# Interleaving the three partial products of each output tile in the Strassen-form matmuls of a LoRA + S4D kernel

## The reference, cut to what matters

```python
# layer 0: base product plus a rank-16 adapter that each of the 128 sequences picks
result = jnp.einsum('bsd,od->bso', x, base_weight) + base_bias      # 1024 x 1024 weight
h = jnp.einsum('bsd,brd->bsr', x, lora_A_w[ids]); result += jnp.einsum('bsr,bor->bso', h, lora_B_w[ids])
x = x + result
# layer 1: per head a causal convolution over the 1024 positions, plus a skip, masked by length
K = 2.0 * jnp.einsum('hn,hnl->hl', Ct, jnp.exp(P)).real
y = irfft(rfft(x, 2048) * rfft(K, 2048))[..., :1024] + x * D[:, None]
x = x + y * mask
```

## Time and profile before

| | |
|---|---|
| median of 3 runs | 1070.05 us (1069.75 to 1071.53) |
| the profiled execution's own time | 1069.73 us |
| its span, first to last instruction | 1068.0 us |
| granted clock of TensorE, mean | 1.000 |
| PE busy | 1061.2 us (99%), 8088 matmuls |
| PEld busy (overlaps PE) | 1028.8 us, 8088 loads |
| DVE busy | 848.5 us (79%) |
| ACT busy | 717.0 us (67%) |
| HBM traffic | 284.62 MB by DMA, mean 266 GB/s |

### The profile page before, as it was taken

The page is one execution under the profiler, slowest core; times in us unless marked ns, Lnnn a source line. Parts: engine busy times, 40 slices in busy tenths (PEclk is TensorE's granted clock), DMA queues, the critical chain, the costliest instruction groups (busy, mean ns, idle before and its releaser), DMA issues.

```text
span 1068.0 us, 21568 instructions
## 1 busy us (share of the span) xinstructions
PE 1061.2 (99%) x8088; PEld 1028.8 (96%) x8088; DVE 848.5 (79%) x1263; ACT 717.0 (67%) x1260; POOL 28.6 (3%) x79
## 2 busy tenths in 40 slices
PE   9999999999999999999999999999999999999998
PEld 7999999999999999999999999999989999999997
DVE  7899887878698787878778787877488888888886
ACT  5755545755747466556557467465598888888885
POOL 0000000000000000000000000000010000000000
PEclk9999999999999999999999999999999999999999
DMA  8586758688786978868785888858798978798873
GB/s 290 202 304 221 275 191 284 199 300 307 226 269 211 298 225 277 282 229 275 229 308 179 296 260 259 293 194 283 264 346 286 350 287 335 294 326 317 304 263 123
DMA packets 162586, 284.62 MB, mean 266 GB/s; under 512 B 10739, under 2 KB 125620, under 8 KB 149044
## 3 DMA queue, kind: packets, MB, share of 16 engines
q1 hardware_dynamic: 162484, 283.26, 77.1%
HBM read 193.96 MB, written 89.26 MB: 265 GB/s over the span
## 4 chain that ended last, share of the span: by engine, by line
PE 97%; DVE 1%; ACT 1%; DMA 0%; issue 0%; DVEq 0%; SPq 0%; ACTq 0%
PE acc L1810 37%; PE acc L1970 25%; PE acc L1816 18%; PE acc L1738 5%; PE acc L1782 5%; PE acc L2005 3%; PE acc L1748 2%; DMA x_raw<-x_t 0%; PE acc L1915 0%; ACT x_hi L687 0%; PE acc L1774 0%; DVE x_sb L1262 0%; ACT L845 0%; ACT L851 0%; DVE g_sb L1460 0%
## 5 line engine op out<-in xcount | busy, mean ns | idle before, releaser
L1970 PE MATMUL acc<-u_hi,f_hi 128*128 128x512 f32 (+1 forms) x320 | 128.9, 403 | 0.0
L687 ACT ACTIVATE acc<-acc 128x512 f32<-128x512 f32 x93 | 54.0, 581 | 109.4 <-PE acc L1816 109.3
L1810 PE MATMUL acc<-t_hi,v_lo 128*128 128x256 f32 x512 | 123.0, 279 | 0.0
L1810 PE MATMUL acc<-t_hi,v_hi 128*128 128x256 f32 x512 | 122.9, 279 | 0.0
L1810 PE MATMUL acc<-t_hi,w_pair 128*128 128x256 f32 x960 | 122.4, 279 | 0.0
L1970 PE MATMUL acc<-u_lo,f_hi 128*128 128x512 f32 (+1 forms) x320 | 118.4, 370 | 0.0
L1970 PE MATMUL acc<-u_hi,f_lo 128*128 128x512 f32 (+1 forms) x320 | 118.2, 369 | 0.0
L1810 PEld LDWEIGHTS acc<-t_hi,w_pair 128*128 128x128 f32 x960 | 116.9, 188 | 0.0
L687 ACT ACTIVATE t_hi<-t_raw 128x1024 fp32r<-128x1024 f32 x64 | 67.9, 1061 | 61.7 <-DVE t_raw L1220 33.0
L1105 DVE TENSOR_TENSOR t_lo<-t_raw,t_hi 128x1024 fp32r<-128x1024 f32 x64 | 78.3, 1223 | 34.3 <-ACT t_hi L687 33.9
L1810 PEld LDWEIGHTS acc<-t_hi,v_lo 128*128 128x128 f32 x512 | 96.2, 188 | 0.0
(11 more groups left out here) (205 smaller groups left out, 2673.3 us busy)
## 6 DMA issues: line engine op xcount, KB each, us to landing
w_pair<-weight_scratch SPq DMA_DIRECT2D x71, 1024.0 KB, 6.5
x_scratch<-x_sb SPq DMA_DIRECT2D x32, 1024.0 KB, 6.0
out<-out_sb SPq DMA_DIRECT2D x63, 512.0 KB, 4.8
x_raw<-x_t SPq DMA_DIRECT2D x15, 2048.0 KB, 11.1
u_raw<-x_scratch SPq DMA_DIRECT2D x14, 2048.0 KB, 11.8
wq_raw<-state_scratch SPq DMA_DIRECT2D x16, 1024.0 KB, 8.1
a_raw<-lora_a SPq DMA_DIRECT2D x128, 64.0 KB, 5.7
b_raw<-lora_b SPq DMA_DIRECT2D x128, 64.0 KB, 2.1
```

Of the source, the lines that this page charges most:

```text
L687: return act.activation(dst, src, ACT.Copy)
L1810: pe.matmul(by_row(bank_part(bank, i)), w[:, k, i, :], hi[:, k, :, :], start=opens and i == 0 and k == 0 and s == 0, stop=False, skip_grou ...
L1970: mm = pe.matmul(bank, w, m, start=first and i == 0, stop=last and i == 2, skip_group_check=onto_closed)
```

## The change

`product_hi` and `product_lo` are replaced by one function, `three_products`, which for each output tile and input block issues W_hi by M_hi, W_hi by M_lo, W_lo by M_hi (the order of the helper `products`, line 381 of before). The number of matmuls, their shapes and their operands stay the same. In `t_product` the wait for `c_tlo` now stands ahead of the whole block product, right behind the wait for `c_thi`. In `x_product` no wait moves: its low parts were waited for before the block product already.

```diff
-            def product_hi(bank, w_hi, w_lo, hi, opens):
+            def three_products(bank, w_hi, w_lo, hi, lo, opens):
 
                 for i in range(QT):
                     for k in range(HALF):
-                        for s, w in enumerate((w_hi, w_lo)):
-                            pe.matmul(by_row(bank_part(bank, i)), w[:, k, i, :], hi[:, k, :, :],
-                                      start=opens and i == 0 and k == 0 and s == 0, stop=False, skip_group_check=True)
-
-            def product_lo(bank, w_hi, lo):
-                for i in range(QT):
-                    for k in range(HALF):
-                        mm = pe.matmul(by_row(bank_part(bank, i)), w_hi[:, k, i, :], lo[:, k, :, :],
-                                       start=False, stop=False, skip_group_check=True)
+                        pairs = products((w_hi[:, k, i, :], w_lo[:, k, i, :]), (hi[:, k, :, :], lo[:, k, :, :]))
+                        for s, (w, m) in enumerate(pairs):
+                            mm = pe.matmul(by_row(bank_part(bank, i)), w, m,
+                                           start=opens and i == 0 and k == 0 and s == 0, stop=False, skip_group_check=True)
                 return mm
 
             def x_product(p, g, j, bank, r, c, opens):
                 w_hi, w_lo = weights(p, g, j)
-                product_hi(bank, w_hi, w_lo, block(x_hi, r, c), opens)
-                return product_lo(bank, w_hi, block(x_lo, r, c))
+                return three_products(bank, w_hi, w_lo, block(x_hi, r, c), block(x_lo, r, c), opens)
 
             def t_product(p, g, j, bank, n, opens):
                 w_hi, w_lo = weights(p, g, j)
                 pe.wait_ge(c_thi[n], g + 1)
-                product_hi(bank, w_hi, w_lo, t_hi[:, :, :, HI_SLOT[n], :], opens)
                 pe.wait_ge(c_tlo[n], g + 1)
-                return product_lo(bank, w_hi, t_lo[:, :, :, LO_SLOT[n], :])
+                return three_products(bank, w_hi, w_lo, t_hi[:, :, :, HI_SLOT[n], :], t_lo[:, :, :, LO_SLOT[n], :], opens)
```

## The result

The changed kernel takes 1074.62 us (median of 5, 1074.34 to 1076.58) against 1070.06 us for the kernel before (5 runs): ratio 1.0043, 95% interval [1.0033, 1.0054]. It is slower by 4.6 us. The forecast was 1072.9 us and slower. Its own range, with the pace unchanged, was 1071.8 to 1074.0, and the measured time lies 0.6 us above that; the whole range, with the rivals in it, went to 1075.4.

A forecast was written before the change was run, and what follows sets the result against it. PE, busy 99%, was taken as the bound: stalls of 1.42 + 0.22 + 1.24 us and pace change 0 make 2.88 us, giving a median of 1072.9 us. Own range 1071.8 to 1074.0; 8-in-10 range 1069.4 to 1075.4.

The forecast's parts named there:

- PE is the bound and nothing later absorbs: Whole kernel: PE, busy 99% of the span, bounds it throughout; only waits PE has anyway can absorb what it loses.
- Loads and repeated weights: All block products: loads stay at 8088, and the second use of a weight is neither loaded less nor paced faster.
- Three stalls, 2.88 us: PE waits for late `t_lo`: 1.42 us at T2 of group 0, 0.22 and 1.24 at T4 of groups 1 and 6.
- The later stalls move with DVE: T4 of groups 1 and 6: DVE's timetable is tied to PE, moves back 1.42 us too, so both lags stay.
- Rival A: Groups 1 and 6: DVE not tied to PE, later stalls absorbed; 1.42 us in all, median 1071.5 us; chance 0.22.
- T4 of group 0 and all others lie far enough ahead: Remaining T products: `t_lo` ends 0.30 us ahead at T4 of group 0, 0.78 or more elsewhere; 0 us.
- Pace change 0: All 5208 matmuls: start-to-start time stays as before, since line 1782 shows 117.5 ns with repeated weights; 0 us.
- the bounds that I had kept: Pace of matmuls: +2.5 us if low T matmuls slow to 117.5 ns, -10.5 us if all others reach 115 ns.
- rival C: T products: low matmuls lose their 115 ns by standing between high ones; +2.5 us, 1075.4 us; chance 0.13.
- My own sign of being wrong: Matmul pace on PE: the prediction is wrong outright if it moves by more than 0.5 ns.
- The signs: Profile after: T2 of group 0 starts about 42.0, group 4 products take 2.8 us, DVE idles near 1.85 us before T4.
- Rival B: All products: repeated weights speed up the pace, by 4.3 to 10.5 us, giving 1068.6 or 1062.4 us; chance 0.11.

## Why the prediction was right, point by point

- *PE is the bound and nothing later absorbs.* Right as far as shown. Before had two stalls on weight loads (0.26 us each, at 363.4 and 600.2) that I had not priced. The run with only the wait moved has neither, and the changed kernel has one. That is no proof that they absorbed a part of the new stalls: the run with only the x products interleaved, where PE loses nothing ahead, also lacks the first and has 0.06 us of the second. The runs with the three late products in the old order have 0.6 us (old slots), and 1.2 and 0.6 us (exchanged slots). What moves these stalls was not tested.
- *Loads and repeated weights.* Right: 8088 loads, and the run without repeated weights is within 0.7 us in its pace sum.
- *Three stalls, 2.88 us.* Right in place and cause, small in size: 3.07. The price of a stall was taken from one on ACT, release + 0.06 and 0.10 for the second matmul. Behind DVE it is 42.01 - 41.87 = 0.14 and 0.08, 0.22 in all.
- *The later stalls move with DVE.* Right: `t_lo` of T4 ends 1.59 us later in group 1 and 2.35 later in group 6, and both products wait as forecast. Rival A's mechanism (DVE is bound by itself) is refuted.
- *T4 of group 0 and all others lie far enough ahead.* Right: 0.29 ahead costs nothing.
- *Pace change 0.* This is the term that was mis-sized: it measured +1.45 us by the table and +1.8 with all intervals, inside the bounds that I had kept. The three stalls alone would have given 1072.9 to 1073.1, and the measured 1074.62 is within the whole range because rival C's term widened it. My own sign of being wrong, a pace that moves by more than 0.5 ns, is met for T2, for T4 and for T3 of the odd tiles, and not for the mean of all products (0.3 ns). My step failed in that I asked only whether a repeated weight is cheaper, and read it off a line with another moving tile. The 115 ns of the low matmuls was on the table, and rival C took it for a matter of neighbours. In the new order T2 lost 1.4 ns and T4 0.7 to 1.4, and T3 of the odd tiles won 0.7. The runs with exchanged slots and with the flat layout show that what alternation costs depends on which slots of T the high and the low part lie in. Rival C had the sign and an upper bound (+2.5 us) but not the cause.
- *The signs.* T2 of group 0 starts at 42.01, as forecast (42.0). T2 of group 4 takes 2.85 us and not 2.8, and DVE's idle time ahead of T4 of group 0 is 2.03 and not 1.85.
- *Rival B* did not come true: the x products, a third of whose matmuls now repeat a weight, moved by 0.1 ns or less.

What makes one placement faster than another stays open. Shown is that the pace goes with the placement of T's parts, and that the same product, with the same placement and order, takes one of two paces about 1 ns apart, and that this goes with what stands ahead of it on PE. Whether the placement of the weights or the other engines' accesses count too is not shown.

## What to carry to other kernels

When two loops are merged into one, the later operand's wait moves to the head: compare the end of each producer with the new first use, group by group. Here 3 of 124 were late, by 0.06 to 1.26 us, and made two thirds of the loss. On a kernel where one engine is busy 99% one nanosecond per matmul is half a percent (5208 ns of 1070 us), so an order or a layout is to be judged by the time from start to start of the very operands in question, in their place in the order, not of similar ones.

## What the runs showed of the hardware that was not expected

- The pace of a 256-column fp32r matmul with its own load went with the step of the moving operand: 119.4 to 120.0 ns with columns side by side, 115.5 to 119.3 for products in runs of 4 columns every 8 or 12, 133 to 134 in runs of 4 every 20.
- It depends on the slots in which the moving operands lie: in the changed kernel the mean inner interval was 114.9 to 119.7 ns for the three positions of the loop, by product.
- It went with what PE ran before: with exchanged slots, T2 of the odd tiles took 116.6 ns in the groups with filters and 117.8 in the others; with no repeated weight, S4 of the odd tiles took 116.7 ns in group 2 and 117.8 in group 4.
- After a wait on DVE the first matmul started 0.14 us behind the producer's end, and the second was 0.08 late. After a wait on ACT it was 0.06 and 0.10 in the stall of the earlier trace rows.
- The Trainium skill, "TensorE: Matmul & The Clock Gate", section "Back-to-back issue gap", gives N / 2.4 + 2.5 ns for the isolated matmul, 109 ns for 256 columns; no run here came below 115 ns for a product. The same section lets the load count in the spacing; here a load stood beside every matmul, repeated weight or not.
